# PSUM banks shared by seven graphs in flight, score products in three row groups, and the digraph diagonal on VectorE

## The reference

```python
x = _layernorm(x + _L0_gnn_ref(x, adj, ...))   # 12 heads, masked by adj > 0, + beta * adj
x = _layernorm(x + _L1_gnn_ref(x, adj, ...))   # 2 graph layers with left and right scores
x = _layernorm(x + _L2_gnn_ref(x, adj, ...))   # 2 digraph layers
x = _layernorm(x + _L3_gnn_ref(x, adj, ...))   # 12 heads, adj as additive bias, output projection
# one digraph layer:
u = h @ h.T / temper
delta = softmax(u, axis=-1) * adjacency_matrix
attn = delta / (sum(delta, axis=-1, keepdims=True) + 1e-10)
hl, hs, hr = h @ wl.T + b_l, h @ ws.T + b_s, h @ wr.T + b_r
ctx = (attn * upper) @ hl + diagonal(attn)[..., None] * hs + (attn * lower) @ hr
out = relu(normalised(ctx) * g + beta)
```

## Time and profile before

| | |
|---|---|
| median of 3 runs | 3090.86 us (3088.84 to 3092.55) |
| the profiled execution | 3095.68 us, of which 3093.9 us are the span of its instructions |
| mean granted clock of TensorE | 0.979 of 2.4 GHz |
| PE busy | 2961.7 us, 96% of the span |
| DVE busy | 2503.8 us, 81% |
| ACT busy | 1833.4 us, 59% |
| POOL busy | 1129.4 us, 37% |

### The profile page before, as it was taken

One profiled execution on the slowest core, in us unless ns is written; L12 is line 12 of the kernel. 1 busy time (PEld: TensorE's weight loads), 2 busy tenths in 40 slices (PEclk: granted clock), 3 DMA queues, 4 the chain that ended last, 5 costly groups with the idle time before them and its releaser, 6 DMA issues.

```text
span 3093.9 us, 91346 instructions
## 1 busy us (share of the span) xinstructions
PE 2961.7 (96%) x35008; PEld 2240.0 (72%) x35008; DVE 2503.8 (81%) x8824; ACT 1833.4 (59%) x4885; POOL 1129.4 (37%) x2315
## 2 busy tenths in 40 slices
PE   3799999999999999999999999999999999999985
PEld 2677777777777777777777777777777777777753
DVE  5578888888888888888888888888888888888763
ACT  5456566666566666666656656666666665666542
POOL 1233333343343333334334334333333433333321
PEclk7899999999999999999999999999999999999996
DMA  7233443444444444444444434434444434443322
GB/s 212 49 61 70 77 80 74 75 80 79 70 80 80 69 80 77 71 81 79 72 75 80 79 71 81 79 68 81 78 74 78 78 73 75 80 77 72 65 50 44
DMA packets 804111, 237.84 MB, mean 77 GB/s; under 512 B 771552, under 2 KB 803424, under 8 KB 803552
## 3 DMA queue, kind: packets, MB, share of 16 engines
q1 hardware_dynamic: 796336, 219.42, 39.4%
q10 hardware_dynamic: 7344, 12.58, 1.3%
HBM read 30.54 MB, written 12.58 MB: 14 GB/s over the span
## 4 chain that ended last, share of the span: by engine, by line
PE 88%; DMA 6%; DVE 2%; ACT 2%; POOL 1%; issue 1%; SPq 1%; POOLq 0%; DVEq 0%; ACTq 0%
PE bank L575 11%; PE bank L577 10%; PE bank L576 10%; PE bank L630 8%; PE bank L563 8%; PE bank L565 8%; PE bank L564 8%; PE bank L681 7%; DMA turned<-flat 5%; PE bank L581 3%; PE bank L613 3%; PE bank L676 3%; PE bank L614 2%; PE bank L615 2%; PE bank L645 1%; PE bank L647 1%
## 5 line engine op out<-in xcount | busy, mean ns | idle before, releaser
L563 PE MATMUL bank<-turned,w_hi 128*128 128x128 f16 x4608 | 821.4, 220 | 12.8 <-DVE ab L744 5.1
L565 PE MATMUL bank<-turned,w_lo 128*128 128x128 f16 x4608 | 821.8, 221 | 0.0
L564 PE MATMUL bank<-turned,w_hi 128*128 128x128 f16 x4608 | 821.8, 221 | 0.0
L506 ACT ACTIVATE ab<-bank 128x384 f16<-128x384 f32 (+1 forms) x896 | 436.6, 487 | 636.0 <-PE bank L581 240.7
L575 PE MATMUL bank<-w_hi,turned 128*128 128x384 f16 x2112 | 693.1, 328 | 25.2 <-DMA turned<-flat 23.5
L576 PE MATMUL bank<-w_lo,turned 128*128 128x384 f16 x2112 | 692.9, 328 | 0.0
L577 PE MATMUL bank<-w_hi,turned 128*128 128x384 f16 x2112 | 692.9, 328 | 0.0
L515 ACT ACTIVATE score<-score,small 128x128 f32<-128x128 f32 x1536 | 499.9, 392 | 91.0 <-DVE small L760 73.6
L744 DVE SCALAR_TENSOR_TENSOR ab<-bank,ab 128x384 f16<-128x384 f32 x512 | 276.8, 550 | 251.0 <-ACT ab L506 251.0
L563 PEld LDWEIGHTS bank<-turned,w_hi 128*128 128x128 f16 x4608 | 457.8, 99 | 29.2 <-issue 15.6
L564 PEld LDWEIGHTS bank<-turned,w_hi 128*128 128x128 f16 x4608 | 454.2, 99 | 14.4 <-issue 0.2
(11 more groups left out here) (118 smaller groups left out, 6503.0 us busy)
## 6 DMA issues: line engine op xcount, KB each, us to landing
turned<-flat SPq DMA_TRANSPOSE x960, 2.8
x<-x_dram SPq DMA_DIRECT2D x64, 192.0 KB, 2.6
out_dram<-score SPq DMA_DIRECT2D x64, 192.0 KB, 2.2
adj<-adj_dram SPq DMA_DIRECT2D x64, 64.0 KB, 2.4
z<-w_dram ACTq DMA_DIRECT2D x6, 576.0 KB, 4.3
score<-w_dram ACTq DMA_DIRECT2D x6, 576.0 KB, 6.1
mask<-w_dram ACTq DMA_DIRECT2D x6, 576.0 KB, 4.2
rows<-rows_dram ACTq DMA_DIRECT2D x1, 1920.0 KB, 8.4
```

What stands on the lines that cost most here:

```text
L506: act.activation(dst, src, ACT.Copy, scale=scale / WSCALE).then_inc(proj_hi_done.of(i), 1)
L563: pe.matmul(dst, lhsT=w_hi[:, w, k, cols], rhs=t_hi[u][:, k, :], start=(k == 0), stop=False)
L564: pe.matmul(dst, lhsT=w_hi[:, w, k, cols], rhs=t_lo[u][:, k, :], start=False, stop=False)
L565: last = pe.matmul(dst, lhsT=w_lo[:, w, k, cols], rhs=t_hi[u][:, k, :], start=False, stop=(k == DT - 1 and w not in BIAS_OF))
```

## The change

What it does, part by part:

- **Slots and banks.** Seven graphs are in flight. The eight PSUM banks belong to no slot: each PE step gets a bank from a pool (`bank(name, k, i)`), and waits (`bank_is_read`) until the reader of what the bank held is done.
- **Order.** `TIMES` goes. `plan()` runs when the program is built: a table `PARTS` of 185 parts, each with a priority, a cost, a delay and the parts it depends on, and a rule that gives each engine the ready part of lowest priority number. It fixes every engine's list and every step's bank. During the run nothing is decided.
- **Scores.** The weight columns of the q and k projections are permuted on the host, so that the three heads of a step lie in three different groups of 32 partitions. The nine matmuls go to three banks, and the three row groups alternate. In block 3 the low half moves from DVE to POOL.
- **Digraph layers.** The identity is no longer in the product: PE makes two f32 products where it made three. DVE takes the diagonal of delta with one more reduction and adds diagonal times `proj[u][1]` to the bank's contents, into SBUF, ahead of the statistics.
- **Start.** Weights have staging tiles of their own, and the first seven graphs may be loaded 10 us apart.

```diff
-UNITS = 8
+UNITS = 7
+BANKS = 8
...
-PERIOD = UNITS * 44.578
-TIMES = {
-    ("load", 0): {SYNC: 0.06},
...
+PERIOD = 42.378
+PARTS = {
+    (PE, "attend", 0): (0.00, 0.234, 0.454, ((SYNC, "scores", 0),), ()),
+    (SYNC, "load", 0): (77.13, 0.900, 3.045, (), ((VECTOR, "residual", 3),)),
...
+def plan():
...
+            able = [max(t, free[engine], freed[BANKS_OF.get(part[1], 1) - 1][0] if engine == PE else 0.0)
+                    for _, part, _, t in ready[engine]]
...
+        if engine == PE:
+            taken = [b for _, b in freed[:BANKS_OF.get(part[1], 1)]]
+            banks[part[1], part[2], i] = taken, [holder[b] for b in taken]
...
+BANKS_OF = {"scores": DT}
+ORDER, BANKS_AT = plan()
...
+            def bank_is_read(i, name, k):
+
+                for holder in BANKS_AT[name, k, i][1]:
+                    if holder is None:
+                        continue
+                    (_, read_by, n), j = holder
+                    if read_by == "project":
+                        pe.wait_ge(*(proj_hi_done if READ_BY["project"](n)[0] == SCALAR else proj_lo_done).at(j, "made", n))
+                    elif read_by == "scores":
+                        pe.wait_ge(*topped.at(j, DT - 1, n))
...
             def scores(i, s):
                 u, g = i % UNITS, s % HG
-                if g == 0:
-                    pe.wait_ge(*proj_lo_done.at(i, "made", L0_K if s < HG else L3_K))
-                else:
-
-                    pe.wait_ge(*topped.at(i, DT - 1, s - 1))
-                if g > 1:
-                    pe.wait_ge(*scalar_done.at(i, "o", s - 2))
-                head = slice(HD * g, HD * g + HD)
-                for t in range(DT):
-                    for qp, kp, n in ((a_hi, b_hi, 0), (a_hi, b_lo, 1), (a_lo, b_hi, 2)):
-                        last = pe.matmul(banks[u][:, t * N:(t + 1) * N], lhsT=qp[u][head, t, :], rhs=kp[u][head, t, :],
+                for w in (L0_V, L0_Q, L0_K) if s < HG else (L3_V, L3_Q, L3_K):
+                    pe.wait_ge(*proj_lo_done.at(i, "made", w))
+                bank_is_read(i, "scores", s)
+
+                for qp, kp, n in ((a_hi, b_hi, 0), (a_hi, b_lo, 1), (a_lo, b_hi, 2)):
+                    for t in range(DT):
+                        group = (g + t) % HG
+                        head = slice(HD * group, HD * group + HD)
+                        last = pe.matmul(bank("scores", s, i, t)[:, 0:N], lhsT=qp[u][head, t, :], rhs=kp[u][head, t, :],
                                          start=(n == 0), stop=(n == 2))
...
-                    for m in range(3):
-                        last = pe.matmul(wide[u], lhsT=delta3[u][:, m, :], rhs=proj[u][m], start=(m == 0), stop=(m == 2))
-                    last.then_inc(multiplied.of(i), 1)
+                    pe.matmul(made[:, 0:D], lhsT=triangles[u][:, 0, :], rhs=proj[u][0], start=True, stop=False)
+                    pe.matmul(made[:, 0:D], lhsT=triangles[u][:, 1, :], rhs=proj[u][2], start=False, stop=True)\
+                      .then_inc(multiplied.of(i), 1)
...
+                dve.wait_ge(*mixed_out.at(i, "delta_di", layer))
+                dve.tensor_tensor_reduce(out=e[u], in0=delta[u], in1=ident, scale=1.0, scalar=0.0, op0=ALU.mult,
+                                         op1=ALU.add, accum_out=col(u, DIAGONAL)).then_inc(numbers.of(i), 1)
...
+                if k >= 2:
+                    dve.wait_ge(*numbers.at(i, "diagonal", k - 2))
+                    dve.scalar_tensor_tensor(zc[u], proj[u][1], col(u, DIAGONAL), src, ALU.mult, ALU.add)\
+                       .then_inc(numbers.of(i), 1)
+                    dve.wait_ge(*numbers.at(i, "summed", k))
+                    src = zc[u]
...
+            def scores(i, s):
+                u = i % UNITS
+                pool.wait_ge(*cast.at(i, "p", s))
+                pool.tensor_tensor(flat[u][:, 1, :], score_at[u], flat[u][:, 0, :], ALU.subtract).then_inc(low_made.of(i), 1)
```

591 lines of the change are left out of this document (375 added, 216 removed).

## The result

The changed kernel takes 2989.55 us in the median (2985.38 to 2990.55), the kernel before 3090.15; the ratio is 0.967 (0.965 to 0.969). I had said 2876 with a range to 2990: faster was right, but of the 214 us that I had forecast only 101 came, and the time stands at the very end of the range. The profiled run took 2990.55 us, its span 2988.8.

What follows compares the result with a forecast made beforehand. PE was taken to set the pace, with 41.5 us of work plus 0.8 of waits per graph. Start 256 + 56.1 * 42.3 + end 250 = 2879 us of span, a 2876 us median; range 2815 to 2990.

Steps and rivals of the forecast that it cites:

- The start: From the beginning to graph 0's last residual sum: 256 us, between 248 and 272.4.
- the end: From graph 63's beginning to the end of the run, its whole chain: 250 us, 245 to 260.
- the middle: PE work between graph 0's last sum and graph 63's beginning: 56.1 graphs at 42.3 us, 2373 us.
- Score step: Nine score matmuls on PE fall from 0.605 to 0.26 us; eight steps per graph give -2.76 us.
- The pace of before: Distance between two stores in the kernel before, taken as PE's time per graph: 45.58 us.
- Identity product: One f32 product fewer on PE in each of two digraph layers: -1.33 us per graph, counting in full.
- Waits: PE's waits, added to its 41.5 us of work per graph: 0.8 us (2%), between 0.1 and 2.8.
- rival C: Lateness at the seam and on DVE: 43.8 us per graph, 2963 us, range 2920 to 3000; chance 0.22.
- DVE and POOL: Loads per graph: DVE 38.4 us, at most 40, including +0.5 for blocking by POOL; POOL 21.2 us.
- Seam: A slot's next graph loads only behind the last residual sum; cover shrinks from 51 to 8 us, so PE sometimes waits.
- B: Score matmuls in three row groups don't overlap: PE needs 44.25 us per graph, 3008 us in all; chance 0.09.
- E: PE stops for banks chosen at build time: slower than before from 46.1 us per graph, 3092 us; chance 0.05.

Runs made afterwards that it cites:

- the other order: The changed kernel with the same operations, its planner's due times and period searched anew against an event model: 2854.25 us, ratio to before 0.923.
- the searched orders: Orders from the event-model search: two of the changed kernel's operations, 2854.25 and 2870.07 us, and one with block 3's low halves back on DVE, 2920.32 us.
- the time left out on DVE: The changed kernel, same lists, with the low halves of both value projections made on one column of each head only: 2988.15 us, ratio to before 0.966.
- the two fast orders: The changed kernel's operations in two orders from event-model searches begun at different due times: 2854.25 us and 2870.07 us.

## Why the prediction was right and wrong

The sum was 256 + 56.1 * 42.3 + 250 = 2879 us of span. Measured in the same pieces: graph 0's last sum at 261.2, then 56.1 * 44.58 = 2501, and what is left to the end, 226.6. The start was 5 us off, the end 23 too high, the middle 128 too low, or 2.28 us per graph:

- *Score step, mis-sized at both ends.* I took 0.605 us for the old and 0.26 for the new. A step of before that stands by itself does take 0.608, near; but four of the eight stand in pairs, at 0.45 to 0.56 apiece, and the mean over 386 steps, start to start, is 0.568. The new one costs 0.285. So 2.26 us instead of 2.76: 28 us.
- *The pace of before*, read from one pair of stores, 45.58; over 40 graphs it is 45.74. 9 us.
- *Identity product*: 1.33 forecast. The digraph mix went from 4.08 to 2.84 us per graph, so 1.24: 5 us.
- *Waits, the step that failed.* I added 0.8 us to PE's work. Between 500 and 2700 us (49.4 graphs) PE waits 82.7 us, 1.67 per graph, where it was 0.16 (idle time alone: 67.1 and 5.7 us); 0.47 per graph go to the half clock. The three terms above leave 86 us, or 1.5 us per graph, for this one; waits and half clock, less the 0.8, account for 1.2 of it, and what is left shows as no wait: it is spread over small delays between matmuls.

5 + 128 - 23 = 110, the gap between 2879 and 2988.8.

**Where the argument failed.** The step that failed is "I add 0.8 us (2%)". I summed each engine's work, saw that the fullest was PE, and gave the interlocking of five fixed lists a lump. I had even written that "the order has the seam's path in it", as evidence against rival C. The order of the changed kernel was there to be read blind: the planner's own times put its loads 36 to 50 us apart and its graphs 42.87 us apart, where `PERIOD` asks for 42.378 and my sum had 42.3 with all waits in it. The experiments say how much was open: the same instructions take 2854, 2870, 2990, 2997 or 3075 us. That the best of them, 42.39 us per graph and 2854 in all, comes near my 42.3 and 2876 is in part luck. By the measured sizes PE's work is 45.74 - 2.26 - 1.24 = 42.2 us, not 41.5; my work was too small by about as much as my lump of waits was too large for that order, and the end some 25 us too long.

**DVE and POOL.** By load they are as forecast: DVE 665.34/775 * 44.58 = 38.3 us per graph (38.4 said), POOL 21.6 (21.2). The mutual lengthening is real: without the reads of POOL's low halves DVE does 37.0 us per graph, 1.2 less. I priced what more of it there would be at half a microsecond of *load* and found it harmless, as DVE was under 95%. Together with the shorter POOL step of those runs it is worth 49 us in changed and 25 in the other order; its own price is not shown. (One reading of rows 8 is loose: the long L813 ends at 1544.42, 0.15 us behind L403, not with it.)

**Seam.** Not the place. PE idles 1.8 us of 775 for a transpose at L776, where a new graph's first tile is read among others, and 9.6 at the attend step, inside a graph. The cover of 8 us that I had worried about held.

**Rivals.** B is shown wrong by starts 3 ns apart and by the run with one row group, and the two kinds of pairs in the trace of before could have told so. C (43.8 us per graph, 2963, chance 0.22) is nearest: right in kind, lateness, and too small; of its two places the seam was wrong, and it left the clock out. E did not happen here, but one number of the planner would have made it (46.18 us per graph; I had put the edge at 46.1). The chances of the sign were right; that forecast and C were 0.56 to 0.22 was not earned by a row.

**What stays open.** How much of the 128 us the clock alone costs was not tried by itself. The price of POOL's reads without its shorter step needs a POOL step that writes only and lasts 0.95 us from its first start to its last end. And in the searched orders lists and banks changed together; only the small waits for banks in changed (7 of 83 us) speak for the lists. Nor is it fully settled why the time left out on DVE brought nothing where the chain runs 23% over DVE: the chain runs over this step 30 times of 128, so 0.37 us less at each could have given 11 us at most.

## What to carry to other kernels

Where every engine follows a fixed list, the time is not the fullest engine's work plus a little: look first at the pace that the planner itself gets, then run the planned order in a model with the durations and handovers of a trace, before and after. A step's price is its start-to-start distance over hundreds of cases among its usual neighbours, not a row in which it stands alone; the cases that fall out of line may show what the change will do. When a control is to keep an engine as long as it was, measure the step from its first start to its last end, not a count times a mean. When a change moves the time less than its work, search the order before undoing the change; here 135 us lay in a table of due times, more than the whole change had brought.

## What the runs showed of the hardware

A wait of PE can cost more than its length: after 2.70 and 1.47 us of standing within 5 us the granted clock was 0.51 (the level of 1.2 GHz) for 6.8 us, two f32 matmuls took 1.62 us instead of 0.89, and f16 matmuls of 384 columns behind them came 320 ns apart instead of 162. In changed that came nine times from 711 to 2500 us, once per cycle of five graphs; in the two fast orders not once between 500 and 2500 us.

Matmuls of 128 columns with 32 contracted rows in three row groups, each with a bank of its own, start 3 ns apart, and the next round comes 57 ns later (medians). From the first to the ninth start are 0.129 us, and then 0.146 us pass until the first full-height matmul behind them starts. The serial form has 0.462 us and the same 0.146. So the row groups take 0.33 us from a step of 0.608, and the edge of about 0.15 us stays. The Trainium skill, "TensorE: Matmul & The Clock Gate", Part 3, counts about 4 ns for each further tile of such a group, and the trace agrees (3 ns).

A GpSimd instruction that only writes SBUF (memsets, 151 ns for 64 columns, 178 for 96) leaves DVE's two-operand instructions at their undisturbed 546 to 559 ns. Such memsets overlap each other: six of 64 columns took 0.58 us, four of 96 columns 0.53.
